# Mixture of experts beside attention on one core: each expert tile scatters its results to token order, and plain loads replace the gathers

## The reference

```python
x = x + 0.5 * ffn(layernorm(x))       # phase 0
x = x + linear_attention(layernorm(x))  # phase 1
x = x + 0.5 * ffn(layernorm(x))       # phase 2, the same weights as phase 0

def ffn(x):
    h = layernorm(x, ln1);  x = x + causal_softmax_attention(h)   # 16 heads of 8
    h = layernorm(x, ln2)
    scores = h @ gate_w                                           # 8 experts
    the two best experts of each token, softmax over the two scores
    out = sum over both of  prob * ((silu(h @ w1[e]) * (h @ w2[e])) @ w3[e])   # 128 -> 256 -> 128
    return x + out
```

## Time and profile before

| | |
|---|---|
| median of 3 runs | 1556.45 us (1554.82 to 1571.91) |
| profiled execution | 1561.33 us |
| its span, first to last instruction | 1559.6 us |
| mean granted TensorE clock | 0.852 of full |
| PE busy | 1065.8 us (68%) |
| DVE busy | 1098.9 us (70%) |
| ACT busy | 763.8 us (49%) |
| POOL busy | 957.6 us (61%) |
| DMA | 98.03 MB, 63 GB/s in the mean |

### The profile page before, as it was taken

The page is one execution under the profiler, slowest core; times in us unless marked ns, Lnnn a source line. Parts: engine busy times, 40 slices in busy tenths (PEclk is TensorE's granted clock), DMA queues, the critical chain, the costliest instruction groups (busy, mean ns, idle before and its releaser), DMA issues.

```text
span 1559.6 us, 37774 instructions
## 1 busy us (share of the span) xinstructions
PE 1065.8 (68%) x12652; PEld 814.7 (52%) x12652; DVE 1098.9 (70%) x2212; ACT 763.8 (49%) x1025; POOL 957.6 (61%) x1079
## 2 busy tenths in 40 slices
PE   5778888888347753786666659888888883477500
PEld 4666666666236642563444438666666662366400
DVE  7868999999524534886777768789999995255322
ACT  3557666666224431455555527666666662244300
POOL 6534477878855557726666652244787888455576
PEclk9899999999669996886666659989999996799855
DMA  8801111111012221201111100011111110122232
GB/s 307 360 19 41 36 47 46 50 47 50 26 53 83 83 70 49 59 12 43 52 50 52 50 11 17 17 36 35 47 50 47 50 47 28 55 86 83 69 79 72
DMA packets 136202, 98.03 MB, mean 63 GB/s; under 512 B 41840, under 2 KB 128752, under 8 KB 133808
## 3 DMA queue, kind: packets, MB, share of 16 engines
q1 hardware_dynamic: 127920, 80.08, 17.0%
q0 software_dynamic: 8192, 16.79, 3.7%
HBM read 24.45 MB, written 40.50 MB: 42 GB/s over the span
## 4 chain that ended last, share of the span: by engine, by line
PE 28%; DVE 24%; issue 16%; POOL 11%; DMA 9%; SPq 6%; ACT 5%; DVEq 1%; POOLq 0%; ACTq 0%
POOL n_all L1310 6%; PE banks_t L389 3%; SPq L1409 3%; PE banks_t L285 3%; DVE negm L873 3%; DMA p_lo<-xy 3%; DMA kst<-k_all 3%; DVE negm L877 3%; DMA pf<-xy 3%; POOL xy L1203 3%; DVE p_lo L886 3%; PE banks_n L495 2%; PE banks_n L267 2%; PE banks_t L396 2%; PE banks_n L369 1%
## 5 line engine op out<-in xcount | busy, mean ns | idle before, releaser
L1253 POOL TENSOR_TENSOR p_lo<-pf,p_hi 128x512 f16<-128x512 f32 x128 | 166.1, 1298 | 209.6 <-ACT p_hi L617 208.8
L600 ACT ACTIVATE pf<-banks_t 128x1536 f32<-128x1536 f32 x128 | 185.6, 1450 | 108.8 <-PE banks_t L396 80.1
L389 PE MATMUL banks_t<-qst,kst 128*128 128x512 f16 x480 | 190.2, 422 | 3.1 <-ACT pf L600 2.1
L617 ACT CAST p_hi<-pf 128x1536 f16<-128x1536 f32 x128 | 188.7, 1474 | 1.1
L873 DVE TENSOR_REDUCE negm<-banks_n 128x4 f16<-128x1024 f32 x128 | 156.1, 1219 | 35.8 <-PE banks_n L369 27.9
L1203 POOL DMA_INDIRECT xy<-n_all,slot x128 | 148.9, 1163 | 27.5 <-issue 25.2
L886 DVE TENSOR_TENSOR p_lo<-pf,p_hi 128x1024 f16<-128x1024 f32 x128 | 162.1, 1266 | 4.9 <-ACT p_hi L617 4.1
L396 PEld LDWEIGHTS banks_t<-ident,negm 128*128 128x128 f16 x1536 | 121.7, 100 | 81.2 <-issue 10.1
L396 PE MATMUL banks_t<-ident,negm 128*128 128x128 f16 x1536 | 152.3, 223 | 0.0
L1310 POOL DMA_INDIRECT n_all<-xy,slot x128 | 124.4, 972 | 45.3 <-issue 37.7
L1292 POOL TENSOR_TENSOR p_lo<-pf,p_hi 128x512 f16<-128x512 f32 x78 | 90.2, 1156 | 95.7 <-DVE p_hi L1075 94.4
(11 more groups left out here) (187 smaller groups left out, 2961.3 us busy)
## 6 DMA issues: line engine op xcount, KB each, us to landing
xy<-qst SPq DMA_DIRECT2D x18, 1024.0 KB, 26.3
qst<-q_all SPq DMA_DIRECT2D x384, 32.0 KB
kst<-k_all SPq DMA_DIRECT2D x96, 128.0 KB
xy<-p_hi SPq DMA_DIRECT2D x78, 128.0 KB, 1.8
v_hl<-v_all SPq DMA_DIRECT2D x96, 68.0 KB, 2.1
pf<-xy SPq DMA_DIRECT2D x40, 128.0 KB, 2.1
p_lo<-xy SPq DMA_DIRECT2D x38, 128.0 KB, 2.1
n_all<-L_ffn_w SPq DMA_DIRECT2D x4, 512.0 KB, 7.5
```

Source lines behind the costliest of these rows:

```text
L389: ins = nc.tensor.matmul(banks[:, c, :], kst[:, g, tk * P:(tk + 1) * P], qst[:, g, :, tq * P:(tq + 1) * P], start=True, stop=not ph["soft" ...
L600: nc.scalar.activation(pf[:, g % 2, :, :, :].rearrange(flat), banks_t[:, :, :].rearrange("p a b -> p (a b)"), ACT.Exp, scale=HD ** -0.5).t ...
L617: nc.scalar.copy(p_hi[:, g % 2, :, :, :].rearrange(flat), pf[:, g % 2, :, :, :].rearrange(flat))\
L1253: nc.gpsimd.tensor_tensor(p_lo[:, g % 2, 2, :, :].rearrange(flat), pf[:, g % 2, 2, :, :].rearrange(flat), p_hi[:, g % 2, 2, :, :].rearrang ...
```

## The change

1. `xy` becomes two DRAM tensors. `xs` holds what `scatter` writes: rows of 130 floats (RW), the 128 of the token and two more, 2 × (its number) and its first choice of expert. They are scattered with the row (520 bytes, not 512). `ys` has one row per (token, choice) in token order, and behind them rows for the entries of a tile that hold no token.
2. In the experts DVE computes for each tile where its 256 results go (`address`): 2 × token + (1 if the tile's expert isn't the token's first choice), or a row behind the end where the entry is beyond the expert's count. POOL then sends y with two indirect DMAs to `ys` (`send`). SP's stores are gone, and its loads wait only for the tile four before (turned and addressed). `y_out` and `dest` have four buffers (YB). `x_low` and `hid_low` move from POOL to DVE, and the high part of `hid` from DVE to ACT (`hid_high`).
3. `gather` goes. SP loads a batch's four row sets with one plain DMA of 256 KB (`load_y`), in a ring of four batches.
4. The routing moves up: `place_of`, `slots` and `scatter` work on batch b − 3 in place of b − 4 and b − 5. `mark` leaves POOL; `choose` on DVE makes `chosen` and copies the first choice into the row. `back_rank` stands behind `values` in its step on PE.
5. The tables get six more DVE operations (`invalid`), the constants three more iotas on POOL, and the first clearing of the DRAM rows goes in pieces of 15 × 128 rows and not 16 × 128.

The diff, cut to its core:

```diff
+XB = 4
+YB = 4
+RW = P + 2
 ...
                     turned(ph, b, g)
-                    if ph["soft"] and g == 1 and place > 3:
-                        back_rank(ph, b - 4)
                     if g < 2 and place > 0:
                         values(ph, b - 1, g + 2)
+                    if ph["soft"] and g == 1 and place > 2:
+                        back_rank(ph, b - 3)
 ...
                 def y_read(t):
                     sc.wait_ge(m["down_done"], t + 1)
+                    if t >= YB:
+                        sc.wait_ge(m["y_kept"][t % YB], 32 * (t // YB))
+                    nc.scalar.copy(y_out[:, t % YB, :, :]..., y_banks[t % 2][:, 0:TS]).then_inc(m["y_in"], 1)
+
+                def hid_high(t):
+                    sc.wait_ge(m["hid_in"], t + 1)
                     if t >= 2:
-                        sc.wait_ge(m["y_kept"][t % 2], 16 * (t // 2))
+                        sc.wait_ge(m["down_done"], t - 1)
+                    nc.scalar.copy(hid_hi[:, t % 2, :], hid[:, t % 2, :]).then_inc(m["hid_hi_in"], 1)
 ...
                     if t >= 2:
                         y_read(t - 2)
+                    hid_high(t)
 ...  (DVE, choose)
+                nc.vector.tensor_copy(n2_all[:, two, P + 1], topi[:, :, 0])
 ...
+                ve.wait_ge(ph["top_in"], b + 1)
+                nc.vector.tensor_tensor(chosen[:, :, :], onehot2[:, b, :, 0, :], onehot2[:, b, :, 1, :], ALU.add)\
+                    .then_inc(ph["chosen_in"], 1)
 ...
-                    if ph["soft"] and g == 1 and place > 3:
-                        place_of(ph, b - 4)
+                    if ph["soft"] and g == 1 and place > 2:
+                        place_of(ph, b - 3)
 ...  (DVE, experts)
+                def address(t):
+                    if t >= YB:
+                        ve.wait_ge(m["y_kept"][t % YB], 32 * (t // YB))
+                    c.link(nc.vector.scalar_tensor_tensor(dest_f[:, t % YB, :], x_nat[t % XB][:, :, P + 1], tab_f[:, 0, t:t + 1],
+                                                          x_nat[t % XB][:, :, P], ALU.not_equal, ALU.add))
+                    nc.vector.tensor_tensor(dest[:, t % YB, :], dest_f[:, t % YB, :], invalid[:, t, :], ALU.max)\
+                        .then_inc(m["dest_in"], 1)
 ...
                 full(0)
+                address(0)
+                x_low(0)
                 for t in range(NTI):
                     if t + 1 < NTI:
                         full(t + 1)
+                        address(t + 1)
+                        x_low(t + 1)
                     product(t)
+                    if t:
+                        hid_low(t - 1)
+                hid_low(NTI - 1)
 ...  (POOL, one batch of the attention loop)
-                    if ph["soft"] and g == 0 and place > 5:
-                        scatter(ph, b - 6, 3)
-                    if ph["soft"] and g == 0 and place > 4:
-                        slots(ph, b - 5)
-                    if ph["soft"] and g and place > 4:
-                        scatter(ph, b - 5, g - 1)
-                    if ph["soft"] and g == 2 and place > 1:
+                    if ph["soft"] and g == 2 and place > 2:
+                        slots(ph, b - 3)
+                    if ph["soft"] and g == 3 and place > 1:
                         keep_n2(ph, b - 2)
-                    if ph["soft"] and g == 2 and place > 2:
-                        mark(ph, b - 3)
+                    if ph["soft"] and g < 2 and place > 3:
+                        scatter(ph, b - 4, g + 2)
+                    if ph["soft"] and g >= 2 and place > 2:
+                        scatter(ph, b - 3, g - 2)
 ...  (POOL, experts)
+                def send(t):
+                    gp.wait_ge(m["y_in"], t + 1)
+                    gp.wait_ge(m["dest_in"], t + 1)
+                    for h in range(2):
+                        nc.gpsimd.indirect_dma_start(ys, bass.IndirectOffsetOnAxis(ap=dest[:, t % YB, h:h + 1], axis=0),
+                                                     y_out[:, t % YB, h, :], None).then_inc(m["y_kept"][t % YB], 16)
 ...  (POOL, front of the linear phase)
-                    gather(mixtures[0], 0)
-                    for pair in range(1, PAIRS):
-                        gather(mixtures[0], pair)
-                        front_rstd(ph, pair - 1)
-                    front_rstd(ph, PAIRS - 1)
+                    for pair in range(PAIRS):
+                        front_rstd(ph, pair)
 ...  (SP)
                     if t >= XB:
                         sy.wait_ge(m["x_turn"], t - XB + 1)
+                        sy.wait_ge(m["dest_in"], t - XB + 1)
 ...
-                for t in range(XB):
+                for t in range(NTI):
                     load(t)
-                for t in range(NTI):
-                    if t + XB < NTI:
-                        load(t + XB)
-                    store(t)
+                for i in range(YB):
+                    sy.wait_ge(m["y_kept"][i], 32 * len(range(i, NTI, YB)))
+
+            def load_y(m, b):
+                if b >= RING:
+                    sy.wait_ge(m["added"], b - RING + 1)
+                sy.dma_start(y_got[:, b % RING, :, :, :],
+                             ys[2 * T * P * b:2 * T * P * (b + 1), :].rearrange("(t p k) d -> p t k d", t=T, k=2))\
+                    .then_inc(m["y_got"][b % RING], 16)
 ...
+                if n == 0:
+                    for b in range(B):
+                        load_y(mixtures[0], b)
+            for b in range(RING):
+                load_y(mixtures[1], b)
             for pair in range(PAIRS):
                 sy.wait_ge(mixtures[1]["added"], BR * (pair + 1))
+                for b in range(BR * pair + RING, BR * (pair + 1) + RING):
+                    if b < B:
+                        load_y(mixtures[1], b)
```

More of the change, by code:

```diff
@@ L38 @@
 ROWS = (E - 1) * CAP + NTI * TS
-ZN = -(-ROWS // (16 * P))
+ZR = 15
+ZN = -(-ROWS // (ZR * P))
 XB = 4
+YB = 4
+RW = P + 2
 RING = 4
@@ L208, in build @@
         mixtures = [dict(**sems(f"m{n}", "x_turn x_hi_in h2f_in x_lo_in up_done silu_in hid_in hid_hi_in hid_lo_in down_done "
-                                "y_in tabled added add_chain e_in chain"),
+                                "y_in dest_in tabled added add_chain e_in chain"),
                          x_loaded=[sem(f"x_loaded_m{n}_{i}") for i in range(XB)],
-                         y_kept=[sem(f"y_kept_m{n}_{i}") for i in range(2)],
+                         y_kept=[sem(f"y_kept_m{n}_{i}") for i in range(YB)],
                          y_got=[sem(f"y_got_m{n}_{i}") for i in range(RING)]) for n in range(2)]
@@ L228, in fill_no @@
                 return 2 * b + ("b1", "b3").index(name)
[L229 to L235, removed]
+            if name in ("b1", "b3") and isinstance(b, int) and b == 0:
+                return ("b1", "b3").index(name)
+            if name == "rank" and isinstance(b, int) and b == B - 1:
+                return 5 * b + 4
+            return 5 * b + {"b1": -1, "b3": 0, "b6": 2, "b8": 3, "rank": 6}[name]
         @block.tensor
@@ L1032, in experts @@
                 c = Chain(ve, m["chain"], 0)
+                ve.wait_ge(consts, 4)
                 def tables():
@@ L1171, in keep_n2 @@
                 apart(gp)
-                flat = "p a b -> p (a b)"
-                nc.gpsimd.tensor_copy(n2_all[:, 2 * b:2 * b + 2, :].rearrange(flat), n2[:, :, :].rearrange(flat))\
-                    .then_inc(ph["n2_kept"], 1)
-            def mark(ph, b):
-                gp.wait_ge(ph["top_in"], b + 1)
-                if b:
-                    gp.wait_ge(ph["filled"], fill_no(ph, b - 1, "rank") + 1)
-                nc.gpsimd.tensor_tensor(chosen[:, :, :], onehot2[:, b, :, 0, :], onehot2[:, b, :, 1, :], ALU.add)\
-                    .then_inc(ph["chosen_in"], 1)
+                nc.gpsimd.tensor_copy(n2_all[:, 2 * b:2 * b + 2, 0:P], n2[:, :, :]).then_inc(ph["n2_kept"], 1)
             def slots(ph, b):
@@ L1314, in attention @@
+                for t in range(NTI):
+                    send(t)
             def attention(ph):
@@ L1364, in _ @@
                     experts(mixtures[n // 2])
-            for pair in range(PAIRS):
-                gather(mixtures[1], pair)
         @block.sync
```

147 lines of the change are left out of this document (70 added, 77 removed).

## The result

The changed kernel takes 1571.52 us (median of 12 runs, 1561.99 to 1578.08); the kernel before took 1559.52 in the runs beside it (1554.82 to 1571.91). The ratio is 1.0069, 95% interval 1.0041 to 1.0097: slower by 0.7%, where 1520 us had been forecast. The profiled execution took 1572.96 us with a span of 1571.2, 11.6 more than before.

The account below looks back on a forecast made before the run. DVE was taken to bound softmax attention, POOL's scatters and gathers the tails and end, and no full engine the experts. Terms −26 + 10 + 54 − 17.6 − 57 = −36.6 us gave 1525 profiled, 1520 us forecast; range 1480 to 1563.

Parts of the forecast that it names:

- The tails: Last row scatters after each softmax attention core: earlier routing saves 13 us each, −26 for both; bounds 10 and 15 each.
- The attention core: Softmax attention: index copy and chosen sum on DVE add 0.35 to 0.45 us a batch, +10 us in all.
- the ring: Experts: address waits on DVE until tile t−4 has landed, so four buffers cover two steps, not four.
- the pace: Experts: 3.95 us a tile, making a stage 159.7 us against 133, +27 each, +54 in all.
- the edges: Expert stage: about 15 us to the release of address(4), 6.5 from last address to last y, 3.9 to landing.
- a loop of 7.7 us: Experts: from one release of address to the landing that releases address(t+2), two tiles; taken as 7.9 with held-up sends.
- Linear front: Start of the linear phase: plain loads replace gathers and rstd waits shorten, −17.6 us in all; bounds −10 and −22.
- end: Last stretch of the kernel, gathers replaced by plain loads: 86.6 us become 30, −57; bounds −48 and −61.
- The first: Rival, experts: the new wait never decides, about 3.05 us a tile, −12 a stage, total near 1442; chance 0.08.
- the third: Rival, experts: both indirect DMAs held up by DVE, landing 3 us, 4.5 a tile, +37, total 1557; chance 0.12.
- The second: Rival, experts: TensorE's clock falls to 1.2 GHz, 0.98 us more a tile, +66, total 1586; chance 0.10.
- The weighed rule of the Trainium skill: Experts: by it DVE's hid_low does not delay sends, loop 7.7 and total 6 us less; the forecast went against it.

## Why the prediction was wrong

**The tails, right.** -11.5 each, foretold -13: the slots and four scatters of a batch are 8.0 and 7.3 us apart here and not the 6.79 of the earlier trace rows, since an rstd and a copy of n2 stand between them.

**The attention core, the step that failed.** It said: "DVE is the bound in some 14 of 16 batches, so +5 us a phase", with bounds 0 and +20. Measured: +22.7 and +21.3, above the upper bound too. With +5 there, the kernel would have come out near 1537. The operations' own length was about right (the block grew by 0.54 us, the kernel with the operations and a late h2 pays 0.3 a batch). What was wrong is the rule behind it, that with DVE as the bound only its own added time counts. DVE was the bound with 1.3 us idle in a batch of 19.1, and the runs show two things on top of its own added time.

First, operations of DVE are held up beside POOL. The upper bound had named this ("if scatters that now run beside earlier batches hold DVE up"), but the sum put it at nothing. The three long batches with a held-up `chosen` and `yb` are 10.6 of the 16.9 us that ten batches gained, and POOL's new order costs as much with the mark back on POOL (1569 us; there `n` is held up in every batch).

Second, the sum had no term for PE. There a turn stands behind the emptying of a bank by DVE, so a later `base` makes scores late, and DVE, the bound, waits for them: 5.0 us in those ten batches, 2.3 before. I asked who is late of the rank alone ("DVE asks for it only at the end of the same group, after a p_low, so nothing is late"), and not who waits for DVE to be done with the bank.

That the core's cost comes from the order and the two operations is shown (old order, 270 and 274 us; new order with the mark on POOL, 292 and 291; old order with the operations, 286 and 289), and so is that curing both the late turn and the held-up sum takes it away (268 and 271). How much of it each of the two has in the changed kernel isn't shown: every edit that moves a step also changes which operations are held up.

**The experts: the ring right, the pace right by luck, the edges undersized.** "Four buffers cover two steps, not four" fits four, five and eight buffers (3.99, 2.86 and 2.74 us a tile, mean of both stages) and the waits of DVE before `address`. But 3.95 was made of a loop of 7.7 us and 0.2 for held-up sends, and neither came so: the sends took 0.96 to 0.98 us on average, most loops at full clock are 7.4, and what brings the mean to 3.97 is longer loops, most of them at a granted clock of 0.8 to 0.92, for which the sum had no term. (The two tenths are 6.8 us in all and not the 6 of the prediction.) Of the first stage, `address(4)` is released at 473.16, 14.9 us after its start (foretold 15); the 34 steps to `address(38)` at 608.98 take 135.8 us, 3.99 each (134.3); from there to the last landing at 622.55 are 13.6 us and not 10.4, because the last three tiles' six sends stand behind one another on POOL:

```profile
613.98 0.96 POOL L1329 DMA_INDIRECT ys<-q_all,dest  x1 [3.25 <-ACT q_all L706]
615.25 0.95 POOL L1329 DMA_INDIRECT ys<-q_all,dest  x1 [0.30 <-issue]
...
620.32 0.96 POOL L1329 DMA_INDIRECT ys<-q_all,dest  x1 [0.30 <-issue]
```

In the second stage a tile took 4.02 us, some 2 us more in all.

**Linear front and end, right.** -18.7 for -17.6, -57.9 for -57; at the end eight pairs of adds need 18.85 us of the 29, and 216 GB/s pass.

**The rivals.** The first (the wait never decides) and the third (sends held up in each loop) did not happen: the 156 sends took 0.97 us on average. The first was also priced too low: by the prediction's own terms a stage at 3.05 us a tile takes 15 + 34 × 3.05 + 10.4 = 129 us, 4 less than before and not 12, a total near 1458. The second happened at most in small: 0.92 was granted in the first expert stage and 0.94 in the second, and the longer loops lie mostly where the clock was lower, but the +66 us of stages at half clock throughout didn't come. In the core the clock fell too, where I had not looked for it.

**Scatters and DVE.** The weighed rule of the Trainium skill ("SBUF — State Buffer", section "Who interferes with whom": a `tensor_tensor` does not stall descriptor generation) made no difference in the experts: it agrees with the sends, which took 0.98 us on average beside DVE's subtractions and 0.96 without. It doesn't agree with 12 of the 128 scatters of the kernel after, which took 1.8 to 1.9 us, each with a subtraction of DVE beside it; most others beside one took about 1.07. The reverse was dearer: operations of DVE, also of one SBUF operand (`yb`, `n`), held up for 0.8 to 2.1 us.

## What to carry to other kernels

A bound engine with 5 to 7% of idle time is not a fixed price per microsecond: before adding to it or moving its steps, list who waits for each step that will come later, and whether that one's lateness returns to it. If two engines take turns at one bank, put work that needs no bank ahead of the wait. Count a ring of buffers in steps from the overwrite to the last reader's landing: one buffer too few cost 88 us here. And read the parts of a loop even where its sum comes out right: 3.97 for 3.95 us a tile hid two terms that were off in opposite directions.

## What the runs showed of the hardware that was not expected

- TensorE's granted clock in the first core (160 to 380 us) was 0.98 to 1.00 in the kernels whose steady batches take under 19.3 us and 0.90 to 0.94 in the others. How late `base` comes doesn't decide it alone: in the kernel after, with PE idle for 1.59 us ahead of the turn and `base` 12.72 us after yb each time, the turn was done at the lower level (1.2 GHz, matmuls of 0.63 us) in the batch of 293.64 and at the upper (2.4 GHz, 0.38) in those of 211.38 and 313.92. I can't say from these runs what decides it.
- An operation of DVE that begins while POOL issues an indirect DMA can be held up past that issue and through the POOL subtraction behind it: 0.20 us became 1.94, and 1.22 became 3.02. When that operation was taken away, the next one to stand there was held up in its place. Which pairs collide was not mapped; the order with the least of it was found by trial, and even there `n` takes 1.38 us in place of 0.60.
